# A TensorE warm-up, one lag moved to TensorE, late weights split earlier and a variance in column strips: a one-core residual block on Trainium2

## The chip, the cores and the metric

The kernel runs on one core of one Trainium2 chip. The time is the device time of one execution in microseconds (us). Three executions of the kernel before are given, and one further execution was profiled. TensorE (PE) multiplies, VectorE (DVE), ScalarE (ACT) and GpSimd (POOL) do the elementwise work, SyncE (SP) issues nearly all DMAs.

## The reference

The input x is 32 batches of 32 tokens with 256 channels, cond is 32 x 256. Two blocks follow each other:

```python
x = x + causal_depthwise_conv(x, w=cond)        # 32 taps (lags 0..31), one 256-wide tap per row of cond
ada = cond @ ada_w + ada_b                      # shift1, scale1, gate1, shift2, scale2, gate2
x1 = ln(x) * (1 + scale1) + shift1              # ln: mean and variance over 256 channels
attn_out = attention(x1 @ qkv_w + qkv_b)        # 16 heads of 128, 32 tokens per batch
y = x + gate1 * (attn_out @ out_w + out_b)
h = gelu((ln(y) * (1 + scale2) + shift2) @ ffn_w1 + ffn_b1)
return x + y + gate2 * (h @ ffn_w2 + ffn_b2)
```

## The kernel before

Channels lie on partitions: two channel tiles (`ct` 0 and 1) of 128 channels, and 1024 tokens in columns, in two halves of 512. The first half is handled in two quarters of 256 tokens through the first layer norm (`CHUNKS`, norms 0 and 1); norm 2 is the second half, norms 3 and 4 belong to the second block. Every engine has its own program written out by hand, and semaphores tie them together.

**Opening.** GpSimd makes the identity `ident` and the constant tile `ones` (1/256). TensorE transposes cond (L896), then the first half of x as it lands (L903); ScalarE and VectorE copy the transposes to `x0`. The convolution of a half is split: the lags in `PE_LAGS` go to TensorE as a product of x with a diagonal matrix of the tap (L917), the rest to VectorE as multiply-adds (L584). A lag j covers 16*(32-j) columns of a half. For the first half TensorE has lags 14 to 31 in the order 14, 31, 15, 30, ... 22, 23 and VectorE lags 0 to 13. The diagonals are made by ScalarE (L379) and GpSimd (L300). Each float32 product shows as two matmul instructions in the trace. Between lags TensorE also transposes the second half of x (L1093), makes the first modulation product (L969), and transposes the biases and the modulation rows. `conv_sum` (L598) adds TensorE's part to VectorE's; from it hang the mean, the squares, the variance, the reciprocal root (L316, a power on GpSimd), its spread over partitions (L961), and the first projection.

**Norm of a quarter.** TensorE's `var(n)` for n < 2 multiplies the squares, as weights, with a column of ones (L945); VectorE adds EPS (L628), GpSimd takes the power of a 128 x nt tile (L316), TensorE's `spread(n)` makes one product per 128 tokens. For n >= 2 the variance is made in strips of 32 partitions (L950), VectorE transposes 32 x 32 blocks (L630), adds EPS (L633), GpSimd takes the power of 128 x 4, and the spread is four products.

**Units.** Eight units U (two halves times four groups of four heads) follow: TensorE projects q, k, v (`project`), makes scores, attends with the probabilities of the unit before (`attend`, L1068) and projects out (`out_proj`). Weights are float32 split into a high part (ScalarE, `high_parts`, L374) and a low part (GpSimd, `low_parts`, L306). In unit 7 the weights of the feed-forward part are split the same way; the last two pieces (`late_raw`, held in `yacc`) are rounded by ScalarE after `exps(7)` (L503) and their low part is made by GpSimd after its loop over the units (L343). Then come `ffn1` and `ffn2`; ScalarE makes the gelu and `hh`, GpSimd and VectorE the low parts `hl` (L348, L843).

Of the kernel before, what the change touches and what calls it, by code (L numbers as in the profile page):

```python
# [5 lines left out]
F32 = mybir.dt.float32  # L6
F32R = mybir.dt.float32r
ALU = mybir.AluOpType
ACT = mybir.ActivationFunctionType
AX_X = mybir.AxisListType.X  # L10

P = 128
HALVES = 2
EPS = 1e-6


def cond_resid_block_kernel(nc, x, cond, ada_w, ada_b, qkv_w, qkv_b, out_w, out_b,
# [5 lines left out]
    B, T, C = x.shape  # L23
# [34 lines left out]

    PE_LAGS = [[lag for pair in zip(range(14, 23), range(31, 22, -1)) for lag in pair], list(range(14, 17))]
    DVE_LAGS = [[j for j in range(T) if j not in lags] for lags in PE_LAGS]
    DIAG_LAGS = PE_LAGS[0]
    ND = len(DIAG_LAGS) * CT
# [6 lines left out]
    with ExitStack() as ctx:  # L71
# [215 lines left out]
        @block.gpsimd  # L287
        def _(g):
            g.memset(ident[:, :], 0.0).then_inc(s_id0, 1)
            g.wait_ge(s_id0, 1)  # L290
            g.affine_select(out=ident[:, :], in_=ident[:, :], compare_op=ALU.not_equal, fill=1.0,
                            base=0, pattern=[[-1, P]], channel_multiplier=1).then_inc(s_const, 1)
            g.memset(ones[:, :], 1.0 / C).then_inc(s_const, 1)
            g.memset(mhalf[:, :], -0.5).then_inc(s_const, 1)
            g.wait_ge(s_const, 3)

            g.wait_ge(s_cond, 1)
            for d, ct in BY_POOL:
                j = DIAG_LAGS[d]
                g.tensor_scalar(diag[:, CT * d + ct, :], ident[:, :], condT[:, ct, T - 1 - j:T - j], 0.0,  # L300
                                ALU.mult, ALU.add).then_inc(s_diag[1], 1)

            def low_part(U, p):
                i, cols = p // 2, slice(PIECE * p, PIECE * (p + 1))
                g.wait_ge(s_whi[i], 2 * U + p % 2 + 1)
                g.tensor_tensor(wl[:, cols], raw[:, cols], wh[:, cols].bitcast(F32), ALU.subtract)\  # L306
                    .then_inc(s_wlo[i], 1)

            def low_parts(U, i):
                low_part(U, 2 * i)  # L310
                low_part(U, 2 * i + 1)

            def rstd(n):
                nt = NORMS[n][1] // P
                g.wait_ge(s_ve, n + 1)
                g.tensor_tensor(rs[:, 0:nt], ve[:, 0:nt], mhalf[:, 0:nt], ALU.pow).then_inc(s_rs, 1)  # L316


            g.wait_ge(s_in, CT)
            low_parts(0, 0)  # L320
            rstd(0)
            low_part(0, 2)
            g.wait_ge(s_lo, CT)
            low_part(0, 3)
            low_part(0, 4)
            rstd(1)
            low_part(0, 5)
            low_parts(0, 3)
            g.memset(pt[:, :, :, :], 0.0).then_inc(s_zero, 1)
            for i in range(3):  # L330
                low_parts(1, i)
            for U in range(1, NU):
                if U == 3:
                    rstd(2)
                if U == 5:
                    rstd(3)
                low_parts(U + 1, 0)
                low_parts(U + 1, 1)
                low_parts(U, 3)
                low_parts(U + 1, 2)  # L340
            for i in range(CT):
                g.wait_ge(s_latehi, i + 1)
                g.tensor_tensor(late_lo[:, i, :], late_raw[:, i, :], late_hi[:, i, :].bitcast(F32), ALU.subtract)\  # L343
                    .then_inc(s_latelo, 1)

            def hidden_low(n, m):
                g.wait_ge(s_hhi, MT * n + m + 1)
                g.tensor_tensor(hl[:, m, :], hf[:, m % 4, :], hh[:, m, :].bitcast(F32), ALU.subtract)\  # L348
                    .then_inc(s_hlo[0], 1)

            for m in (0, 2):
                hidden_low(0, m)

            g.wait_ge(s_mlo, CT * 3)
            for m in (4, 6):
                hidden_low(0, m)
            rstd(4)
            for m in (0, 2, 4, 6):
                hidden_low(1, m)

        @block.scalar
        def _(a):
# [85 lines left out]
            def o_high(U, h):  # L448
                a.wait_ge(s_pv, GH * U + h + 1)
                a.activation(oh[:, h, :], OB[h % 2][:, :], ACT.Identity, bias=bias(U, 2, h)).then_inc(s_ohi, 1)  # L450
# [21 lines left out]
            for U in range(1, NU):  # L472
                for j in range(4):
                    evac(U, j)
                if U == 1:

                    a.wait_ge(s_adap, 3)
                    a.wait_ge(s_adax, 1)
                    a.activation(ada_rows[:, :], S_BANK[:, 0:2 * P], ACT.Copy).then_inc(s_adac, 1)
                o_high(U - 1, 0)  # L480
                o_high(U - 1, 1)
                if U == 3:
                    squares(2)
                if U == 5:
                    squares(3)
                evac(U, 4)
                o_high(U - 1, 2)
                high_parts(U + 1, 0)
                o_high(U - 1, 3)
                if U == 3:  # L490
                    x1_high(2)
                if U == 5:
                    x1_high(3)
                for j in (5, 6, 7, 8):
                    evac(U, j)
                    if U in (2, 4) and j in (6, 7):
                        mean_high(U // 2 + 1, j - 6)
                high_parts(U + 1, 1)
                exps(U)
                if U == NU - 1:  # L500
                    a.wait_ge(s_late, 16 * CT)
                    for i in range(CT):
                        a.activation(late_hi[:, i, :], late_raw[:, i, :], ACT.Copy)\  # L503
                            .then_inc(s_latehi, 1)
                evac(U, 9)
                high_parts(U, 3)
                evac(U, 10)
                evac(U, 11)
                high_parts(U + 1, 2)
# [41 lines left out]
        def _(v):  # L551
# [71 lines left out]

            def var_eps(n):
                v.wait_ge(s_var, n + 1)
                if n < 2:
                    nt = NORMS[n][1] // P
                    v.tensor_scalar(ve[:, 0:nt], STAT_BANK[n][:, 0:nt], EPS, None, ALU.add).then_inc(s_ve, 1)  # L628
                else:
                    v.transpose(vt[:, :, :], STAT_BANK[n][:, 0:P].rearrange("p (k r) -> p k r", r=T))\  # L630
                        .then_inc(s_vt, 1)
                    v.wait_ge(s_vt, n - 1)
                    v.tensor_scalar(ve[:, :], vt[:, :, 0:1].rearrange("p k r -> p (k r)"), EPS, None, ALU.add)\  # L633
                        .then_inc(s_ve, 1)

            def norm(n):
                v.wait_ge(s_rb, n + 1)
# [252 lines left out]

        @block.tensor
        def _(pe):
            pe.wait_ge(s_const, 1)
            pe.wait_ge(s_row[0], 16)
            for ct in range(CT):
                m = pe.transpose(S_BANK[:, B * ct:B * (ct + 1)], crow[:, ct * P:(ct + 1) * P], ident[0:B, 0:B])  # L896
# [1 line left out]
            for n in range(2):  # L898
                t0, nt = CHUNKS[n][0] // P, CHUNKS[n][1] // P
                pe.wait_ge(s_x[n], 16)  # L900
                for ct in range(CT):
                    for t in range(nt):
                        m = pe.transpose((OB, YB)[n][ct][:, t * P:(t + 1) * P], xtok[:, t0 + t, ct * P:(ct + 1) * P], ident[:, :])  # L903
                m.then_inc(s_xt, 1)

            def conv(n, i0, i1):
                last = len(PE_LAGS[n]) - 1
# [31 lines left out]

            def var(n):  # L940
                pe.wait_ge(s_sq, CT * (n + 1))
                if n < 2:
                    for t in range(NORMS[n][1] // P):
                        for ct in range(CT):
                            m = pe.matmul(STAT_BANK[n][:, t:t + 1], ln_sq(n, ct)[:, t * P:(t + 1) * P],  # L945
                                          ones[:, 0:1], start=(ct == 0), stop=(ct == CT - 1))
                else:
                    for ct in range(CT):
                        for t in range(TG):
                            m = pe.matmul(STAT_BANK[n][T * t:T * (t + 1), 0:P], ones[:, 0:T],  # L950
                                          ln_sq(n, ct)[:, t * P:(t + 1) * P], start=(ct == 0), stop=(ct == CT - 1))
                m.then_inc(s_var, 1)

            def spread(n):
                pe.wait_ge(s_rs, n + 1)
                for k in range(NORMS[n][1] // P):
                    if n < 2:
                        dst = STAT_BANK[n][:, k * P:(k + 1) * P]
                    else:
                        dst = STAT_BANK[n][:, :].rearrange("p (t k r) -> p k t r", t=TG, r=T)[:, k]  # L960
                    m = pe.matmul(dst, rs[:, k:k + 1].to_broadcast([P, P]), ident[:, :], start=True, stop=True)  # L961
                m.then_inc(s_rb, 1)

            def modulation(i):
# [323 lines left out]
```

## Time and profile before

| what | value |
|---|---|
| three runs | 311.98, 313.19, 313.54 us, median 313.19 |
| profiled execution, its own time | 314.73 us |
| its span, first to last instruction | 312.9 us |
| TensorE busy | 302.3 us, 97% of the span, 2604 matmul instructions |
| VectorE, ScalarE, GpSimd busy | 177.7, 174.4, 119.5 us |
| mean granted TensorE clock | 0.998 |

The profiled execution's time is 1.83 us above its span, and 1.54 us above the median of the three runs. Busy times are sums over the whole span; they don't tell which wait ends last in a stage. The start of an instruction in the timeline is where it begins, and the distance between two starts is what one costs in a dense stream; its own duration also holds a tail that the next one overlaps.

### The profile page before, as it was taken

The page shows a single profiled execution, that of the slowest core. Times are in us where ns is not written, and L with a number is a line of the kernel's source. Part 1 is how long each engine was busy: PE and PEld are TensorE (multiplying, and loading weights), DVE is VectorE, ACT ScalarE, POOL GpSimd, SP SyncE. Part 2 cuts the span into 40 slices and gives each one's busy share as a digit, 9 for nine tenths or more (in the row PEclk, how much of TensorE's full clock was granted, in tenths as well). Part 3 has the DMA queues.
Part 4 walks back from the last instruction along what each step waited for, and adds up shares of the span by engine and source line. Part 5 has one row for each costly group of instructions (what it writes and reads, how often), then busy time and mean ns, then how long its engine had stood idle before and what let it go on. Part 6 is the DMA issues. An engine that isn't in the chain of part 4 may idle for free.

```text
span 312.9 us, 6154 instructions
## 1 busy us (share of the span) xinstructions
PE 302.3 (97%) x2604; PEld 255.2 (82%) x2604; DVE 177.7 (57%) x304; ACT 174.4 (56%) x316; POOL 119.5 (38%) x103
## 2 busy tenths in 40 slices
PE   4998999999999999999999999999999989999995
PEld 3896897887888888888888888888898868878885
DVE  3985798888768555453446553340620555757232
ACT  5454567543762856376367636644762793725901
POOL 5105646630823364064327224630911492311400
PEclk9999999999999999999999999999999999999999
DMA  6902240600080052007003400520180000000012
GB/s 216 374 24 65 71 136 2 196 7 0 3 270 0 2 164 107 1 4 266 3 2 112 159 2 2 180 90 0 33 304 2 2 0 3 0 0 1 2 67 67
DMA packets 15275, 23.00 MB, mean 74 GB/s; under 512 B 808, under 2 KB 8336, under 8 KB 15248
## 3 DMA queue, kind: packets, MB, share of 16 engines
q1 hardware_dynamic: 15200, 22.58, 21.4%
q8 instruction: 20, 0.33, 0.4%
q14 instruction: 7, 0.06, 0.1%
q10 hardware_dynamic: 48, 0.03, 0.0%
HBM read 21.57 MB, written 1.05 MB: 72 GB/s over the span
## 4 chain that ended last, share of the span: by engine, by line
PE 87%; DVE 5%; ACT 4%; POOL 2%; DMA 1%; issue 1%; DVEq 0%
PE bank L981 15%; PE bank L983 15%; PE bank L982 15%; PE bank L1068 8%; PE bank L917 5%; PE bank L989 4%; PE bank L991 4%; PE bank L990 4%; PE bank L1052 3%; PE bank L1191 2%; PE bank L1193 2%; PE bank L1192 2%; POOL wl L306 1%; PE bank L961 1%; ACT wh L374 1%; DVE xc L584 1%
## 5 line engine op out<-in xcount | busy, mean ns | idle before, releaser
L306 POOL TENSOR_TENSOR wl<-raw,wh 128x512 fp32r<-128x512 f32 x70 | 94.9, 1381 | 129.7 <-ACT wh L374 110.9
L425 ACT ACTIVATE pool<-bank,bT 128x512 f32<-128x512 f32 x56 | 38.5, 688 | 54.4 <-PE bank L983 54.4
L981 PE MATMUL bank<-x1h,wl 128*128 128x512 f32 (+1 forms) x174 | 65.6, 377 | 0.5 <-POOL wl L306 0.5
L982 PE MATMUL bank<-x1l,wh 128*128 128x512 f32 (+1 forms) x174 | 64.6, 371 | 0.0
L983 PE MATMUL bank<-x1h,wh 128*128 128x512 f32 (+1 forms) x174 | 64.6, 371 | 0.0
L707 DVE SCALAR_TENSOR_TENSOR ol<-bank,bT,oh 128x512 fp32r<-128x512 f32 x32 | 24.0, 750 | 37.4 <-ACT oh L450 36.3
L584 DVE SCALAR_TENSOR_TENSOR xc<-x,condT,xc 128x496 f32<-128x496 f32 (+27 forms) x82 | 43.3, 597 | 0.1
L374 ACT ACTIVATE wh<-raw 128x512 fp32r<-128x512 f32 x70 | 39.8, 622 | 0.0
L981 PEld LDWEIGHTS bank<-x1h,wl 128*128 128x128 f32 x174 | 32.8, 189 | 6.5 <-POOL wl L306 1.0
L983 PEld LDWEIGHTS bank<-x1h,wh 128*128 128x128 f32 x174 | 32.7, 188 | 5.7
L982 PEld LDWEIGHTS bank<-x1l,wh 128*128 128x128 f32 x174 | 32.8, 188 | 5.3
L1068 PEld LDWEIGHTS bank<-pt,pool 128*128 128x128 f32 x256 | 32.1, 191 | 3.7 <-issue 1.9
L1068 PE MATMUL bank<-pt,pool 128*128 128x128 f32 x256 | 32.5, 275 | 1.5 <-DVE ol L707 1.5
L450 ACT ACTIVATE oh<-bank,bT 128x512 fp32r<-128x512 f32 x32 | 22.0, 687 | 10.9 <-PE bank L1068 10.9
L981 PE MATMUL bank<-oh,wl 128*128 128x512 f32 x64 | 26.7, 418 | 0.2 <-DVE ol L707 0.2
L989 PE MATMUL bank<-wh,x1l 128*128 128x512 f32 x64 | 25.9, 405 | 0.0
L983 PE MATMUL bank<-oh,wh 128*128 128x512 f32 x64 | 25.1, 392 | 0.0
L991 PE MATMUL bank<-wh,x1h 128*128 128x512 f32 x64 | 25.0, 391 | 0.0
L982 PE MATMUL bank<-ol,wh 128*128 128x512 f32 x64 | 25.0, 390 | 0.0
L990 PE MATMUL bank<-wl,x1h 128*128 128x512 f32 x64 | 25.0, 390 | 0.0
L702 DVE STREAM_TRANSPOSE pt<-pnorm 32x512 f32<-32x512 f32 (+1 forms) x36 | 23.2, 644 | 1.2
L679 DVE TENSOR_REDUCE mx<-bank 128x16 f32<-128x512 f32 x8 | 5.5, 692 | 32.2 <-PE bank L1052 32.2
(136 smaller groups left out, 432.4 us busy)
## 6 DMA issues: line engine op xcount, KB each, us to landing
raw<-in_L_cond_qkv_w_dram SPq DMA_DIRECT2D x24, 512.0 KB, 5.6
raw<-in_L_cond_out_w_dram SPq DMA_DIRECT2D x8, 512.0 KB, 3.5
raw<-in_L_cond_ffn_w_dram SPq DMA_DIRECT2D x3, 512.0 KB, 6.2
adaw<-in_L_cond_ada_w_dram SPq DMA_DIRECT2D x1, 1024.0 KB, 10.6
out_dram<-pool SPq DMA_DIRECT2D x3, 256.0 KB, 2.2
xtok<-in_x_dram SPq DMA_DIRECT2D x2, 256.0 KB, 3.1
adaw<-in_L_cond_ada_w_dram SPq DMA_DIRECT2D x1, 512.0 KB, 5.7
xtok<-in_x_dram SPq DMA_DIRECT2D x1, 512.0 KB, 6.5
```

The source lines that it names most:

```text
L306: g.tensor_tensor(wl[:, cols], raw[:, cols], wh[:, cols].bitcast(F32), ALU.subtract)\
L374: a.activation(wh[:, cols], raw[:, cols], ACT.Copy).then_inc(s_whi[i], 1)
L425: a.activation((q_sb if j < GH else k_sb)[:, j % GH, :], src, ACT.Identity, bias=bias(U, j // GH, j % GH)).then_inc(s_ev, 1)
L584: m = v.scalar_tensor_tensor(out=acc[:, :, j:], in0=xs[:, :, :T - j], scalar=w, in1=(acc if i else xs)[:, :, j:], op0=ALU.mult, op1=ALU.add)
L707: v.scalar_tensor_tensor(out=ol[:, h, :], in0=OB[h % 2][:, :], scalar=bT[:, row:row + 1], in1=oh[:, h, :].bitcast(F32), op0=ALU.add, op1=A ...
L981: pe.matmul(dst, wl[:, w_cols], a_hi, start=start, stop=False)
L982: pe.matmul(dst, wh[:, w_cols], a_lo, start=False, stop=False)
L983: return pe.matmul(dst, wh[:, w_cols], a_hi, start=False, stop=stop)
L989: pe.matmul(dst, x1l[:, kt, tk], wh[:, wc], start=(kt == 0), stop=False)
L990: pe.matmul(dst, x1h[:, kt, tk], wl[:, wc], start=False, stop=False)
L991: m = pe.matmul(dst, x1h[:, kt, tk], wh[:, wc], start=False, stop=(kt == CT - 1))
L1068: m = pe.matmul(OB[h % 2][:, t * P:(t + 1) * P], v_sb[:, t, h * P:(h + 1) * P], pt[:, h, t, :], start=True, stop=True)
```

## The change

Four edits: lag 13 of the first half moves from VectorE to TensorE and the order of TensorE's lags becomes 13, 31, 14, 30, 15, ... 23, 22; TensorE makes four products of the constants before the first transposes and three behind the transposes of x, into a bank that is read by nobody then; the late weights are split earlier in unit 7 on ScalarE and GpSimd; norm 1 (the second quarter) takes the variance and its spread by the way of norms 2 to 4.

```diff
-    PE_LAGS = [[lag for pair in zip(range(14, 23), range(31, 22, -1)) for lag in pair], list(range(14, 17))]
+    PE_LAGS = [[13] + [lag for pair in zip(range(31, 22, -1), range(14, 23)) for lag in pair], list(range(14, 17))]
 ...
             def rstd(n):
                 nt = NORMS[n][1] // P
+                at = (slice(0, P), slice(0, nt)) if n == 0 else (slice(0, T * nt), slice(0, TG))
                 g.wait_ge(s_ve, n + 1)
-                g.tensor_tensor(rs[:, 0:nt], ve[:, 0:nt], mhalf[:, 0:nt], ALU.pow).then_inc(s_rs, 1)
+                g.tensor_tensor(rs[at], ve[at], mhalf[at], ALU.pow).then_inc(s_rs, 1)
 ...
                 low_parts(U + 1, 0)
+                if U == NU - 1:
+                    for i in range(CT):
+                        g.wait_ge(s_latehi, i + 1)
+                        g.tensor_tensor(late_lo[:, i, :], late_raw[:, i, :], late_hi[:, i, :].bitcast(F32),
+                                        ALU.subtract).then_inc(s_latelo, 1)
                 low_parts(U + 1, 1)
                 low_parts(U, 3)
                 low_parts(U + 1, 2)
-            for i in range(CT):
-                g.wait_ge(s_latehi, i + 1)
-                g.tensor_tensor(late_lo[:, i, :], late_raw[:, i, :], late_hi[:, i, :].bitcast(F32), ALU.subtract)\
-                    .then_inc(s_latelo, 1)
 ...
                 o_high(U - 1, 3)
+                if U == NU - 1:
+                    a.wait_ge(s_late, 16 * CT)
+                    for i in range(CT):
+                        a.activation(late_hi[:, i, :], late_raw[:, i, :], ACT.Copy)\
+                            .then_inc(s_latehi, 1)
 ...
                 high_parts(U + 1, 1)
                 exps(U)
-                if U == NU - 1:
-                    a.wait_ge(s_late, 16 * CT)
-                    for i in range(CT):
-                        a.activation(late_hi[:, i, :], late_raw[:, i, :], ACT.Copy)\
-                            .then_inc(s_latehi, 1)
 ...
             def var_eps(n):
                 v.wait_ge(s_var, n + 1)
-                if n < 2:
+                strips = T * (NORMS[n][1] // P)
+                if n == 0:
                     nt = NORMS[n][1] // P
                     v.tensor_scalar(ve[:, 0:nt], STAT_BANK[n][:, 0:nt], EPS, None, ALU.add).then_inc(s_ve, 1)
                 else:
-                    v.transpose(vt[:, :, :], STAT_BANK[n][:, 0:P].rearrange("p (k r) -> p k r", r=T))\
+                    v.transpose(vt[0:strips], STAT_BANK[n][0:strips, 0:P].rearrange("p (k r) -> p k r", r=T))\
                         .then_inc(s_vt, 1)
-                    v.wait_ge(s_vt, n - 1)
-                    v.tensor_scalar(ve[:, :], vt[:, :, 0:1].rearrange("p k r -> p (k r)"), EPS, None, ALU.add)\
-                        .then_inc(s_ve, 1)
+                    v.wait_ge(s_vt, n)
+                    v.tensor_scalar(ve[0:strips, :], vt[0:strips, :, 0:1].rearrange("p k r -> p (k r)"), EPS, None,
+                                    ALU.add).then_inc(s_ve, 1)
 ...
-            pe.wait_ge(s_const, 1)
+            def idle_products(count):
+
+                for _ in range(count):
+                    pe.matmul(PB[1][:, 0:P], ident[:, :], ones[:, :], start=True, stop=True)
+
+            pe.wait_ge(s_const, 2)
+            idle_products(4)
 ...
                 m.then_inc(s_xt, 1)
+            idle_products(3)
 ...
             def var(n):
                 pe.wait_ge(s_sq, CT * (n + 1))
-                if n < 2:
+                if n == 0:
 ...
                 else:
                     for ct in range(CT):
-                        for t in range(TG):
+                        for t in range(NORMS[n][1] // P):
 ...
             def spread(n):
                 pe.wait_ge(s_rs, n + 1)
-                for k in range(NORMS[n][1] // P):
-                    if n < 2:
-                        dst = STAT_BANK[n][:, k * P:(k + 1) * P]
+                nt = NORMS[n][1] // P
+                for k in range(nt if n == 0 else TG):
+                    if n == 0:
+                        dst, rows_n = STAT_BANK[n][:, k * P:(k + 1) * P], P
                     else:
-                        dst = STAT_BANK[n][:, :].rearrange("p (t k r) -> p k t r", t=TG, r=T)[:, k]
-                    m = pe.matmul(dst, rs[:, k:k + 1].to_broadcast([P, P]), ident[:, :], start=True, stop=True)
+                        dst = STAT_BANK[n][:, 0:P * nt].rearrange("p (t k r) -> p k t r", t=nt, r=T)[:, k]
+                        rows_n = T * nt
+                    m = pe.matmul(dst, rs[0:rows_n, k:k + 1].to_broadcast([rows_n, P]), ident[0:rows_n, 0:rows_n],
+                                  start=True, stop=True)
                 m.then_inc(s_rb, 1)
```

## Rows read from the trace of the kernel before

**Rows 1.** The page: shares of the chain that ended last, by engine.

```profile
PE 87%; DVE 5%; ACT 4%; POOL 2%; DMA 1%; issue 1%; DVEq 0%
```

**Rows 2.** Timeline of the opening: start us, duration us, engine, line, tiles.

```profile
1.42 0.20 POOL L293 MEMSET ones<- 128x128 f32 x1
6.04 5.36 ACT L379 ACTIVATE diag<-ident,condT 128x128 f32<-128x128 f32 x18
20.67 0.54 DVE L584 SCALAR_TENSOR_TENSOR xc<-x,condT,xc 128x320 f32<-128x320 f32 x1
24.89 0.95 DVE L598 TENSOR_TENSOR xc<-xc,bank 128x144 f32<-128x144 f32 x4 [2.79 <-PE bank L917]
```

**Rows 3.** Timeline of TensorE, 5 to 19 us, single instructions.

```profile
6.33 0.85 PE L917 MATMUL bank<-x,diag 128*128 128x288 f32 x1 [0.60 <-DVE x L564]
7.45 0.69 PE L917 MATMUL bank<-x,diag 128*128 128x288 f32 x1
7.93 0.69 PE L917 MATMUL bank<-x,diag 128*128 128x288 f32 x1
9.12 0.80 PE L917 MATMUL bank<-x,diag 128*128 128x272 f32 x1
14.37 0.44 PE L1093 MATMUL bank<-ident,xtok 128*128 128x128 f32 x1
16.89 0.61 PE L917 MATMUL bank<-x,diag 128*128 128x240 f32 x1
18.32 0.41 PE L917 MATMUL bank<-x,diag 128*128 128x224 f32 x1
```

**Rows 4.** Windows: stretch, busy of each engine (instructions), granted clock, DMA share, GB/s.

```profile
10.00:15.00 5.00, 5.00 (x18) 4.29 (x18) 5.00 (x9) 1.40 (x5) 0.00 (x0) 1.00 1.04 386
```

**Rows 5.** Timeline of TensorE, 19 to 30 us.

```profile
19.64 0.64 PE L969 MATMUL bank<-adaw,condT 128*32 128x128 f32 x16
28.10 1.05 PE L945 MATMUL bank<-ones,x 128*128 128x1 f32 x8 [0.47 <-ACT x L405]
29.56 0.39 PE L917 MATMUL bank<-x,diag 128*128 128x272 f32 x1
29.80 0.39 PE L917 MATMUL bank<-x,diag 128*128 128x272 f32 x1
```

**Rows 6.** Timeline of the second quarter's norm.

```profile
36.28 0.15 DVE L628 TENSOR_SCALAR ve<-bank 128x2 f32<-128x2 f32 x1
36.51 0.70 POOL L316 TENSOR_TENSOR rs<-ve,mhalf 128x2 f32<-128x2 f32 x1 [0.43 <-DVE ve L628]
37.26 0.52 PEld L961 LDWEIGHTS bank<-ident,rs 128*128 128x128 f32 x4 [0.35 <-POOL rs L316]
```

**Rows 7.** Timeline and chain, the same steps in norm 4.

```profile
276.18 0.31 DVE L630 STREAM_TRANSPOSE vt<-bank 128x128 f32<-128x128 f32 x1
276.77 1.01 POOL L316 TENSOR_TENSOR rs<-ve,mhalf 128x4 f32<-128x4 f32 x1 [3.17 <-DVE ve L633]
...
278.56 0.89 PE bank L961 x8
```

**Rows 8.** Timeline of unit 7 and the step into ffn1.

```profile
240.02 0.69 ACT L425 ACTIVATE pool<-bank,bT 128x512 f32<-128x512 f32 x1 [4.76 <-PE bank L983]
245.30 2.56 POOL L306 TENSOR_TENSOR wl<-raw,wh 128x512 fp32r<-128x512 f32 x2 [9.19 <-ACT wh L374]
247.32 1.14 ACT L503 ACTIVATE late_hi<-yacc 128x512 fp32r<-128x512 f32 x2
255.92 1.67 DVE L843 TENSOR_TENSOR hl<-pool,hh 128x512 fp32r<-128x512 f32 x1 [3.03 <-ACT hh L519]
258.40 1.13 PE L1068 MATMUL bank<-pt,pool 128*128 128x128 f32 x8 [1.54 <-DVE ol L707]
275.57 0.69 DVE L843 TENSOR_TENSOR hl<-pool,hh 128x512 fp32r<-128x512 f32 x1 [0.55 <-ACT hh L519]
```

**Rows 9.** Windows (columns as in the windows group above), after the late weights' loads.

```profile
234.00:236.00 2.00, 2.00 (x13) 1.71 (x13) 0.71 (x1) 0.72 (x2) 2.00 (x2) 1.00 0.01 3
```

## The prediction, made before the changed kernel was run

> **What bounds the kernel now.** I read the page first. TensorE is busy for 97% of the span, and of the chain that ended last it holds 87% [rows 1]. So time is won in two ways only: TensorE does less (or does it faster), or it waits less. Next I read its waits. There are few, and two bear on this change: the 1.54 us before the third `attend` of unit 7 at 258.40, put down to VectorE's `ol` [rows 8], and 0.35 us before the spread of the second quarter [rows 6]. Last I read the opening instruction by instruction, because half of the change sits there.
>
> In the opening the reader should compare distances between starts. Two 288-column instructions start 0.48 us apart at 7.45 and 7.93 [rows 3]; two 272-column ones start 0.24 us apart at 29.56 and 29.80 [rows 5]. Per column that is 1.67 ns against 0.88 ns: TensorE runs at its lower level (1.2 GHz) early and at 2.4 GHz later. At 16.89 a 240-column instruction still lasts 0.61 us, at 18.32 a 224-column one lasts 0.41 us [rows 3], so the level rises in between, about 18.0. The granted clock of 10 to 15 us reads 1.00 all the same [rows 4]; for this stretch the durations decide, not that column. The Trainium skill (TensorE: Matmul & The Clock Gate, Part 1) says the lower clock is the default and activity releases it; that agrees with the durations and not with the granted clock.
>
> The opening ends with TensorE: VectorE's last wide multiply-add of lag 12 starts at 20.67, it then does the two of lag 13 (0.46 us each by the distance between such starts), and idles 2.79 us for TensorE until 24.89 [rows 2]. All that follows hangs from `conv_sum`, on every engine, so a shift of it goes through to the end undiminished unless a later wait takes it; the waits left on TensorE are too small to take it.
>
> **Edit 1: products of constants, and lag 13.** The first four products need `ones`, ready at 1.62 [rows 2]; eight instructions of 128 columns at 1.67 ns a column are 8 x 0.213 = 1.7 us, to about 3.4. That is where TensorE starts on cond now. Cost: 0 to 0.1 us. The second group starts when the x transposes are through. The engine was idle for 0.60 us before 6.33 [rows 3], the tail of 0.2 us counts as free too, and six instructions are 1.28 us: the convolution starts at about 6.8 instead of 6.33. Cost 0.5 us at the lower level.
>
> What they may buy is the rise of the clock. Before, it rose inside a dense stretch that began with the transposes at 14.37; in front of it, the wide lags were broken by narrow ones (lag 31, 16 columns, has its four instructions from 7.93 + 0.48 = 8.41 to 9.12, 0.18 us each, in which hardly anything streams) and by the idle 0.60 us [rows 3]. With the change the stretch from 1.7 to 8.8 is dense but for some 0.3 us at 3.5: products, transposes, products, then the 304 columns of lag 13. The longest dense stretch so far is shorter than this one. I let the rise fall at 7.8, one microsecond behind the convolution's new start and well inside the dense part; bounds 5 and 9, its middle and its end.
>
> TensorE's work of the opening at the upper level: the wide lags 13 to 23 have 16 x (19+18+...+9) = 2464 columns per tile; four instructions each at 0.88 ns a column give 8.7 us. The eight narrow lags 24 to 31 go at the floor; eight one-column instructions took 1.05 us with a tail, so 0.12 us each [rows 5], 4 x 0.12 x 8 = 3.8 us. Between them: eight transposes at 0.12 (1.0), the modulation product (0.6) [rows 5], two small turns (0.2). Sum 14.3 us. From 6.8 that ends at 21.1; one microsecond at the lower level in front (to 7.8) does half its work, so 21.6. Here lag 13 itself is 304 x 4 x 0.88 = 1.07 us of TensorE.
>
> VectorE loses the two multiply-adds of lag 13 and is through at 20.67 + 0.54 = 21.2. So TensorE still ends last, at 21.6 against 24.89 before: **-3.3 us**. With a rise at 5, VectorE's 21.2 to 21.3 binds: -3.6. With a rise at 9 it is 22.2: -2.7. ScalarE's diagonals, now 28 for 27, are at hand: 18 of them are made by 11.4 [rows 2], and the last eight follow the second half's copies, some 2.4 us of work behind transposes that come two microseconds earlier. Were they late, TensorE would wait for lags 25 and on; I price that at 0 and name it below.
>
> **Edit 2: the late weights.** ScalarE's two conversions take 1.14 us at 247.32 (1.04 without the tail), in front of the last copies, the conversions of `w2` and the first gelu. Moved behind `o_high(6, 3)` they fall into the 4.76 us in which ScalarE waits before 240.02 [rows 8]. Their loads have landed by then: the DMA moves 3 GB/s from 234 to 236 [rows 9]. On GpSimd the two subtractions leave the place before `hidden_low(0, 0)` and fall into the wait between `low_parts(8, 0)` and 245.30. Two subtractions of their form take 2.56 us there, the wait is 9.19 us [rows 8]. Nothing else queues behind either new place before 240.
>
> Effect on the stall: ScalarE's whole chain comes 1.04 us earlier, and VectorE's `hl` of tile 1, which took 1.67 us at 255.92 beside GpSimd's work and takes 0.69 us alone at 275.57 [rows 8], should take nearer to 0.7. Together up to 2.0 us, more than the 1.54 us of idle at 258.40, so the stall goes: **-1.6 us** (the 0.1 is the start of a stream after a wait). Bounds: -1.0 if only ScalarE's part counts, -1.7. Late next is the projection of head 2, which needs an `ol` with more than 1 us to spare. If the cover before 240 were gone, 1.04 us of ScalarE would hit the copy of tile 5.
>
> **Edit 3: second quarter's variance in strips.** TensorE's own variance product gets cheaper than the 1.05 us of eight one-column instructions (norm 0's, of the same form [rows 5]), but behind it TensorE waits 0.35 us for the reciprocal root anyway [rows 6], so a saving there only lengthens that wait: 0. The path is VectorE, GpSimd, spread. VectorE's EPS ran at 36.28, not because of TensorE but behind its own modulation multiplies. Now a block transpose goes in front. In norm 4 the power starts 0.59 us after the transpose starts [rows 7], here 0.23 us after EPS [rows 6]: +0.36. The power of 128 x 4 takes 1.01 us [rows 7], that of 128 x 2 0.70 [rows 6]; the new one is 64 x 4. Both rows have all partitions, so the cost follows the columns: +0.30, bound 0 from below if 64 partitions cost half. The spread becomes four products of 64 columns, eight instructions; four products of 128 columns took 0.89 [rows 7], two take half of it, 0.45: +0.43, and 0 from below if the narrow ones pair up. Sum **+1.1 us** on the path, bounds +0.3 and +1.2. Behind the spread TensorE streams without a break for 10 us, so nothing absorbs it; the next waits there are for steps that follow TensorE themselves.
>
> **Sum.** -3.3 - 1.6 + 1.1 = -3.8 us. The profiled execution would go from 314.73 to 310.9, its span from 312.9 to 309.1. The profiled time stands 1.54 us over the median; against that median of 313.19 it is **309.4 us**.
>
> **Rivals.** A change of 0.5% (1.6 us) is about what a measurement of this kernel can tell from none.
>
> A, the clock rises no earlier (slower). Durations before show a full 2 us of 288 columns after transposes without a rise. Then six lags at the lower level from 6.8: 864 wide columns x 4 x 1.67 = 5.8, three narrow lags 2.1, to 14.7; transposes 1.7, lag 16 1.7, rise at 18.1; the rest (1344 columns 4.7, five narrow 2.4, others 0.8) ends at 26.0, +1.1 against 24.89, or +2.6 if the rise slips another 3 us. Net +0.6 to +2.1, **314.5 us**. It decides when the rise comes after 15.4: there 21.1 + 8.6/2 = 25.4 eats the 0.5 that edits 2 and 3 leave. Chance 0.13.
>
> B, the rise comes earlier, but only near 12, because the transposes break the stretch. 21.1 + 2.6 = 23.7, -1.2, net -1.7: **311.5 us**. Against it: before, the rise came right behind eight transposes. Chance 0.12. Beside it stands a rule of the Trainium skill (TensorE: Matmul & The Clock Gate, Part 4): a transpose doesn't count as activity. By it the dense part would begin at 5.5 with the second products; the transposes in front of the rise at 18.0 speak against that rule.
>
> C, the stall at 258.40 stays or half stays, since the `ol` behind it waits for something else: net -2.2 to -3.2, **310.5 us**. Chance 0.08.
>
> D, the strips cost nothing (the order of GpSimd's low parts shifts, or the narrow spread is quick): -4.9, **308.3 us**. Chance 0.12.
>
> My forecast keeps 0.55, with its own range 308.4 to 310.4. The range over cases leaves out A and little else: 307.8 to 311.6. Faster by over 0.5% (under 311.6): the forecast, C, D, and half of B, 0.81; within: the other half of B and half of A, 0.12; slower: 0.07.
>
> **What would show it.** Edit 1: starts of TensorE's instructions in lag 13 to 15 spaced 0.25 us instead of 0.5, `conv_sum` near 21.6, VectorE's idle before it under 0.5 us. Edit 2: `late_hi` near 232, no idle before the third `attend` of the last unit, VectorE's `hl` of tile 1 at 0.7 us. Edit 3: a power of 1.0 us and TensorE idle of 1 us or more before the spread, which then takes 0.9 us. I am wrong if the lower level lasts beyond 12 us, if diagonals come late for lag 25 and on, or if another wait grows between 25 and 60 us by what the opening gave.

## The result, and the profile after

| | kernel before | changed kernel |
|---|---|---|
| median of 20 runs | 312.16 us (311.95 to 313.70) | 313.69 us (312.58 to 315.50) |
| ratio to before, over all executions | | 1.0038, 95% interval 1.0022 to 1.0055 |
| profiled execution, its span | 314.73, 312.9 us | 314.52, 312.6 us |

Ratios are taken over all executions, so they differ a little from the quotient of two medians. One execution, 428.0 us at a mean granted clock of 0.657 in the run with two tiny products, was in a slower state, and its ratio leaves it out.

I had forecast 309.4 us in a range of 307.8 to 311.6. The change makes the kernel a little slower. The two profiled spans are equal within 0.3 us, so the first question is whether the forecast gains are there. They are. The timeline of the opening in the changed kernel:

```profile
7.01 0.42 PE L927 MATMUL bank<-x,diag 128*128 128x304 f32 x1
7.26 0.42 PE L927 MATMUL bank<-x,diag 128*128 128x304 f32 x1
21.65 0.98 DVE L600 TENSOR_TENSOR xc<-xc,bank 128x152 f32<-128x152 f32 x4
```

304 columns now cost 0.25 us from start to start, the upper level from the first lag on (it starts at 6.75), where 288 columns took 0.48 [rows 3]. The products of constants just before start 0.21 us apart up to 6.2 us and 0.11 us apart from 6.4 on, so the clock rose at about 6.3. The sum of the convolution starts at 21.65, not 24.89 [rows 2]: 3.24 us earlier. It carries no idle bracket: VectorE, not TensorE, ends last, and TensorE waits for it 1.7 us.

The second quarter's norm, from the same view:

```profile
33.06 0.30 DVE L633 STREAM_TRANSPOSE vt<-bank 64x128 f32<-64x128 f32 x1
33.63 1.00 POOL L317 TENSOR_TENSOR rs<-ve,mhalf 64x4 f32<-64x4 f32 x1 [0.78 <-DVE ve L636]
34.69 1.10 PE L973 MATMUL bank<-ident,rs 64*128 64x64 f32 x8 [1.13 <-POOL rs L317]
```

The answers to [rows 6]: the transpose stands in front, the power takes 1.00 us on half the partitions, as on all of them, TensorE waits 1.13 us for it, and from the spread's start to the next product it is 1.03 us (34.69 to 35.72) where it was 0.47 (37.26 to 37.73). And the last unit:

```profile
236.52 1.14 ACT L495 ACTIVATE late_hi<-yacc 128x512 fp32r<-128x512 f32 x2
237.45 2.52 POOL L342 TENSOR_TENSOR late_lo<-yacc,late_hi 128x512 fp32r<-128x512 f32 x2
256.60 0.69 DVE L846 TENSOR_TENSOR hl<-pool,hh 128x512 fp32r<-128x512 f32 x1 [2.33 <-ACT hh L521]
258.10 1.13 PE L1081 MATMUL bank<-pt,pool 128*128 128x128 f32 x8
```

Against [rows 8], VectorE's `hl` takes 0.69 us instead of 1.67, and the 1.54 us of idle in front of TensorE's third `attend` is gone. ScalarE converts the late weights at 236.52, not near 232 as forecast, but still inside its wait, which shrinks from 4.76 to 3.73 us. Now the place where the gains were lost. In the timeline of TensorE there is a hole in unit 3, two matmuls before the end of the scores:

```profile
131.57 1.28 PE L1065 MATMUL bank<-pool 128*32 128x32 f32 x126
134.79 0.22 PE L1065 MATMUL bank<-pool 128*32 128x32 f32 x2 [1.94 <-issue]
...
162.19 1.30 PE L1065 MATMUL bank<-pool 128*32 128x32 f32 x128
```

The windows of the stretch behind it (busy of each engine, then the granted clock, DMA share, GB/s):

```profile
136.00:138.00 2.00, 2.00 (x7) 1.51 (x5) 1.27 (x3) 1.50 (x3) 0.00 (x0) 0.52 0.00 0
138.00:140.00 2.00, 2.00 (x7) 1.63 (x6) 1.90 (x4) 1.14 (x3) 1.79 (x2) 0.62 0.03 8
```

126 of 128 matmuls run, then TensorE stands for 1.94 us for nothing the profile shows ("issue"), then the last two run. After that wait the granted clock falls to its lower level for some 3.4 us. From these scores to the next unit's it is 30.6 us (131.57 to 162.19); in the kernel before (133.97 to 160.81) and in a later run without a hole it is 26.8. So the hole and the clock behind it cost 3.8 us in this execution. Of the 20 runs, seven had a mean granted clock of 1.0 and took 312.6 to 312.9 us, ten had 0.995 (313.5 to 314.7), three 0.989 (315.4 to 315.5): the clock does not fall every time, and seems to fall twice in some. Where it fell is seen only in the profiled one. The waits of the opening can do the same, as a run below shows, so not every fall need come from the hole.

With the hole in, the two profiles add up. Opening -3.2; strips +0.8 (from the sum of the convolution to unit 1's scores, 53.5 us for 52.7); unit 3 to unit 4 +3.8; from unit 4's scores to the end, with the late weights, -1.7 (150.5 us for 152.1). That is -0.3 us, and the spans are 312.6 and 312.9.

### The profile page after: what moved, and what is told of

The parts are those of the page before. It is cut to its first block, busy times and chain, and to the rows that moved or that the text cites. A ratio compares the mean times of both kernels' runs of the same rounds, so it can differ in the third digit from the quotient of the medians.

```text
span 312.6 us, 6198 instructions
## 1 busy us (share of the span) xinstructions
PE 302.2 (97%) x2626; PEld 255.3 (82%) x2626; DVE 176.2 (56%) x303; ACT 174.5 (56%) x317; POOL 120.0 (38%) x104
## 3 DMA queue, kind: packets, MB, share of 16 engines
HBM read 21.57 MB, written 1.05 MB: 72 GB/s over the span
## 4 chain that ended last, share of the span: by engine, by line
PE 86%; DVE 8%; POOL 2%; ACT 2%; issue 1%; DVEq 0%; POOLq 0%
PE bank L994 16%; PE bank L996 15%; PE bank L995 15%; PE bank L1081 9%; DVE xc L586 5%; PE bank L1002 5%; PE bank L1004 5%; PE bank L1003 5%; PE bank L1065 3%; PE bank L1204 2%; PE bank L1206 2%; PE bank L1205 2%; PE bank L973 1%; POOL wl L306 1%; PE bank L940 1%
## 5 line engine op out<-in xcount | busy, mean ns | idle before, releaser
L586 DVE SCALAR_TENSOR_TENSOR xc<-x,condT,xc 128x496 f32<-128x496 f32 (+27 forms) x80 | 42.1, 595 | 0.1
L994 PE MATMUL bank<-oh,wl 128*128 128x512 f32 x64 | 26.8, 418 | 0.2 <-DVE ol L710 0.2
L1004 PE MATMUL bank<-wh,x1h 128*128 128x512 f32 x64 | 25.7, 402 | 0.0
```

The costliest lines, as they stand in the source:

```text
L586: m = v.scalar_tensor_tensor(out=acc[:, :, j:], in0=xs[:, :, :T - j], scalar=w, in1=(acc if i else xs)[:, :, j:], op0=ALU.mult, op1=ALU.add)
L994: pe.matmul(dst, wl[:, w_cols], a_hi, start=start, stop=False)
L1004: m = pe.matmul(dst, x1h[:, kt, tk], wh[:, wc], start=False, stop=(kt == CT - 1))
```

## The experiments

A *tiny product* below is this, one float32 product into a bank nobody reads then. It stands as four instructions in TensorE's program (two weight loads, two matmuls), so it moves all that follows by four places and takes little time:

```python
pe.matmul(PB[1][0:32, 0:32], ident[:, 0:32], ones[:, 0:32], start=True, stop=True)
```

The kernel before was timed again beside these runs; its medians lie between 312.0 and 312.1 us.

**Two tiny products in front of the first four products (changed kernel otherwise).**

> The changed kernel with two tiny products (128x32 by 32 columns, eight TensorE instructions with their weight loads) put in front of the four products of constants; nothing else. Theory 1, code loading: the 1.94 us hole in unit 3's scores and the lower clock behind it come from a 256-instruction piece of TensorE's code that ends two matmuls before the 256-instruction burst of scores does; eight instructions more put the border inside the burst, so the hole and the clock drop vanish and the span falls by 1.9 to 3.8 us, to about 309 us, device time near 310.7. Theory 2, the products or the strips disturb unit 3 by timing or power: nothing moves, 312.6 to 315.

Median 312.95 us (before: 312.0), ratio 1.0008 (0.9982 to 1.0034). Timeline of its unit 3:

```profile
131.85 1.25 PE L1067 MATMUL bank<-pool 128*32 128x32 f32 x122
134.82 0.26 PE L1067 MATMUL bank<-pool 128*32 128x32 f32 x6 [1.73 <-issue]
```

My size was wrong: the hole stayed, at 1.73 us. Its place was right: eight instructions more in front moved it by four matmuls and their four weight loads. In both kernels it stands in front of TensorE's 1233rd matmul. It sits at a fixed place of the program's code, not at a fixed work step. In this profile the clock did not fall, and to the next scores it is 28.8 us, 1.9 more than without a hole.

**The kernel before with 44 instructions more, and nothing of the change.**

```diff
-            pe.wait_ge(s_const, 1)
+            pe.wait_ge(s_const, 2)
+            for _ in range(11):
+                pe.matmul(PB[1][0:32, 0:32], ident[:, 0:32], ones[:, 0:32], start=True, stop=True)
```

> The kernel before with eleven tiny products (44 TensorE instructions) ahead of the wait for cond; nothing of the change is in it. Theory 1 (code loading): its scores of unit 3 stand where those of the changed kernel stand in TensorE's code, so a hole of 1.9 us appears there, often with a stretch at the lower clock: 1.9 to 3.8 us slower than before. Theory 2: no difference to before beyond 0.3 us, or a small gain if the tiny products raise the clock earlier.

Median 314.88 us against 312.0, ratio 1.0066 (1.0041 to 1.0091); the fastest execution is 2.2 us above the fastest of the kernel before (314.04, 311.81). Timeline:

```profile
131.19 1.28 PE L1054 MATMUL bank<-pool 128*32 128x32 f32 x126
134.41 0.22 PE L1054 MATMUL bank<-pool 128*32 128x32 f32 x2 [1.94 <-issue]
```

The same hole at the same matmul and with the same length, in a kernel with none of the four edits. This settles where the hole comes from: the change's 22 more matmul instructions, each with its weight load (2626 for 2604, so 44 places), are enough, whatever they compute. The page's queue of instructions agrees in size: 20 packets with 0.33 MB in the kernel before, 21 in the changed one, so about 16 KB of code a packet; the 5208 matmuls and weight loads of the kernel before are 20.3 pieces of 256. The Trainium skill (Runtime: NRT & Kernel Launch, Instruction fetch mechanics) says engines refill code in 16 KiB blocks of 256 instructions, which agrees; it also calls the crossing mostly hidden, and of some twenty crossings here one is not. One unit's scores are 256 instructions in 1.3 us. When a border of the pieces lies a few instructions in front of them, the whole next piece is used up before the one after it is there.

The trace also has the time of each packet of that queue. In the four profiles with a hole (this one, the changed kernel, the runs before and after this one) a 16 KB packet starts 0.5 to 0.6 us into the scores of unit 3, and TensorE goes on 2.3 to 2.7 us after its start (132.07 and 134.79 in the changed kernel). In front of unit 4 of the changed kernel the packet starts at 160.66, 1.5 us ahead of the scores, and there is no hole. The unchanged kernel has a packet 0.7 us into unit 3's scores too, but there the 1233rd matmul comes 20 matmuls behind them. That TensorE waits for this packet is read from these times; the profile names no releaser.

**The old variance of the second quarter, four tiny products in front.**

> The changed kernel with the second quarter's variance and spread as before (one-column products, a power of 128x2, two spreading products), and four tiny products in front so that the later code stands exactly as in the run with two tiny products. My theory: the strips cost 1.1 us on the path from the reciprocal root to the spread, so this is 1.1 us faster than that run, near 309.6. Rival: the strips are free or gain, no difference or slower.

Median 312.18 us, ratio 0.9990 (0.9969 to 1.0011), 0.8 us below the run with two tiny products, at the same code place and with the same hole behind 122 matmuls (1.64 us). I had expected 1.1. From the sum of the convolution to unit 1's scores it is 52.7 us here and 53.5 there, 0.8.

**The kernel before with the late weights' edit alone.**

> The kernel before with the late weights' edit alone; TensorE's code is as before. My theory: the 1.54 us idle of TensorE in the last unit goes, 1.5 to 1.7 us faster than before, span 311.3 in a profile like that of before. Rival: half of it stays, 0.8 us.

Median 310.90 against 312.0 us, ratio 0.9945 (0.9922 to 0.9968), which is 1.7 us. The medians are only 1.1 apart, but both the fastest and the slowest executions are 1.7 apart (310.13 and 312.88 against 311.81 and 314.59), and in the profiles it is 150.3 us from unit 4's scores to the end instead of 152.1. The third `attend` of the last unit in its timeline has no idle in front:

```profile
254.10 1.13 PE L1069 MATMUL bank<-pt,pool 128*128 128x128 f32 x8
```

**Eight tiny products behind the three products of constants: the code moves by 32.**

> The changed kernel with eight tiny products behind the three products of constants: TensorE's later code moves by 32 instructions. Theory 1 (code loading): the run with two tiny products moved the hole by exactly four matmuls and kept it, since the piece of code still starts less than 3 us before the scores; with 32 the piece starts about 4 us before them, the hole goes in every unit, 1.9 us less and no lower clock in unit 3: about 310.9 us. Rival: the hole moves again by 16 matmuls and stays near 1.7 us, or another unit gets one: 312.6.

Median 310.86 against 312.09 us, ratio 0.9954 (0.9935 to 0.9973), as expected. The timeline shows the scores of unit 3 whole:

```profile
132.71 1.30 PE L1067 MATMUL bank<-pool 128*32 128x32 f32 x128
```

In its trace no packet of code starts between 124.94 and 134.51. So the changed kernel, with its four edits untouched and its code moved, goes from 313.69 to 310.86: the code's place was worth 2.8 us. The seven executions of the changed kernel without a fall of the clock (312.6 to 312.9) lie 1.9 us above 310.86, which is the hole alone. Four of its twelve runs took 311.8 to 311.9, at a mean granted clock of 0.993 or 0.994. The profile is of one of those, and its windows show where: the granted clock falls behind the two waits of the opening (1.4 us for the sum of the convolution, 1.1 us for the spread of the strips).

```profile
36.00:38.00 2.00, 2.00 (x11) 2.00 (x11) 2.00 (x3) 0.00 (x0) 2.00 (x2) 0.50 0.38 88
```

**The same with the old variance** (ten tiny products; the later code stands at the same place).

> As the run with eight tiny products, with the second quarter's variance and spread as before and ten tiny products, so that the later code stands at the same place. My theory: the strips cost 0.8 to 1.1 us on the path, so about 309.9 us, and below the kernel before by 2 us. Rival: strips free, no difference to the other run.

Median 309.97 us (309.83 to 310.29 in six runs), ratio 0.9916 (0.9885 to 0.9947). The strips cost 0.9 us by the medians.

**The same without the products of constants** (17 tiny ones behind x).

> As the last, without the seven products of constants (tiny products keep the code at its place); lag 13 stays on TensorE. Theory A: the products raise the clock early; without them the convolution runs at the lower level for a time that differs from execution to execution, the sum of the convolution comes between 21.3 and 26, and the times spread over 3 us with a median 1 us or more above. Theory B: the clock rises early in most executions anyway; median equal or 0.3 us lower, since cond and x are transposed 0.3 us sooner.

Median 310.20 us, 309.64 to 310.89, ratio 0.9922. This tells little: the 17 tiny products themselves ran for 1.5 us in the place of the others, and in the profile the clock rose among them, at about 6.6 us (their instructions start 0.053 us apart, then 0.032), before lag 13. It wasn't a kernel without products.

**The same as the run with ten tiny products, lag 13 back on VectorE, old order of lags** (twelve tiny products).

> As the run with the old norm, with lag 13 back on VectorE and the old order of lags: products, late weights and shifted code only. If VectorE bounds the opening once the clock is high, the sum of the convolution comes 0.9 us later (near 22.5) and the time is 0.9 us longer than with lag 13 moved. Rival: TensorE bounds it, no difference.

Median 311.53 us, ratio 0.9979 (0.9956 to 1.0002), 1.56 us more than with lag 13 moved. The sum of the convolution starts at 22.42 instead of 21.74, 0.7 us. The rest is again the clock: TensorE now waits longest, and the mean's products behind that wait run slow (1.54 us where they take 1.10); from 24 to 26 us the windows read 0.50. The one execution of twelve at a mean clock of 0.999 took 310.73, 0.8 above 309.97.

```profile
22.42 0.94 DVE L600 TENSOR_TENSOR xc<-xc,bank 128x144 f32<-128x144 f32 x4
23.09 1.54 PE L948 MATMUL bank<-xc,ones 128*128 128x256 f32 x4 [2.36 <-DVE xc L600]
```

**Three products in front, three behind, eleven tiny ones in the wait before the mean; old variance.**

```diff
-            idle_products(4)
+            idle_products(3)
...
             conv(0, 16, len(PE_LAGS[0]))
+            for _ in range(11):
+                pe.matmul(PB[1][0:32, 0:32], ident[:, 0:32], ones[:, 0:32], start=True, stop=True)
```

> Lag 13 on TensorE, late weights early, the old variance of the second quarter; three products of constants in front instead of four, three behind, and the eleven tiny products that place the code stand in the wait before the mean. With four in front, VectorE's work began 0.3 us later than without; with three TensorE is free when cond lands, so the sum of the convolution comes near 21.4 and the time is 0.2 to 0.3 us below the 309.97 of the run with four, near 309.7. Rival: a shorter dense stretch lets the clock rise later in some executions and the median rises above 310.

Median 309.37 us (309.32 to 309.63 in six runs) against 312.10, ratio 0.9885 (0.9851 to 0.9920): the fastest of all, 1.15% below the kernel before. I had expected 309.7; the sum starts at 21.34, as expected:

```profile
21.34 0.98 DVE L600 TENSOR_TENSOR xc<-xc,bank 128x152 f32<-128x152 f32 x4
```

**No product before the convolution at all** (17 tiny ones in the wait before the mean, otherwise as the last).

> The same without any product of constants before the convolution (in the run that left them out before, seventeen tiny ones stood there and the clock was up by 8). Theory A, the products raise the clock: now the convolution starts at the lower level, which ends anywhere between 9 and 18 us, the sum of the convolution comes at 21.3 to 25, times spread over 309.7 to 313, median 1 us or more above the run with three and three. Theory B, they do nothing: same median within 0.3 us.

Median 312.56 us, from 310.71 to 314.65, ratio 0.9983 (0.9950 to 1.0017): 3.2 us above the run with three and three, and spread over 4 us where that one spreads over 0.3. Its timeline shows the lower level through lag 13 and most of lag 14, and TensorE late:

```profile
7.50 0.71 PE L925 MATMUL bank<-x,diag 128*128 128x304 f32 x1
11.70 0.39 PE L925 MATMUL bank<-x,diag 128*128 128x272 f32 x1
22.27 0.98 DVE L600 TENSOR_TENSOR xc<-xc,bank 128x152 f32<-128x152 f32 x4 [0.95 <-PE bank L925]
```

So the products do what they seem to be for: theory A holds. About 0.5 of the 3.2 us is the tiny products' own, though: TensorE is late here, they stand in the way, and the mean's first product starts 1.28 us behind the sum (22.27 to 23.55) where it was 0.68 (21.34 to 22.02). And the products pay only together with lag 13. Lag 13 moved without products took 312.56, products without lag 13 moved 311.53, and neither of the two, in the run with the late weights alone, 310.90; both together took 309.97 and 309.37. (These runs differ in their tiny products too.) In the seven profiles with six or seven products the clock rose between 5.3 and 7.0 us; in five without, apart from the run with 17 tiny ones in their place, between 10.5 and 18.0.

**The kernel before once more.**

> The kernel before once more for its profile. If the moment at which the clock rises differs from execution to execution, TensorE's convolution in this profile ends near 22.1 to 22.5 instead of 24.8, and the sum of the convolution starts within 0.5 us of VectorE's last multiply-add; span about 310.2. If the first profile was typical, the sum starts at 24.9 again.

```profile
15.82 0.37 PE L917 MATMUL bank<-x,diag 128*128 128x240 f32 x1
23.59 0.95 DVE L598 TENSOR_TENSOR xc<-xc,bank 128x144 f32<-128x144 f32 x4 [1.47 <-PE bank L917]
```

At 16.89 the first profile still had 0.61 us for a 240-column instruction [rows 3]; here it is 0.37 at 15.82. The clock rose some 2.5 us earlier, the sum came at 23.59, and the execution took 313.29 us: 1.44 less than the first profile's 314.73, for 1.30 us of earlier sum. The eight runs took 311.8 to 313.3. Neither of my two numbers was hit; the answer lies between. In the profile of the late weights alone, whose opening is the same, the sum came at 22.49. All 76 executions of the kernel before beside the experiments fall into three groups, 311.8 to 312.4, 313.1 to 313.5 and 314.6 to 314.8 (six of them): the first profile belongs to the slowest.

## Why the prediction was wrong

**What failed is a step that isn't in it.** The prediction priced what each edit adds or moves in time, and said that a shift of `conv_sum` "goes through to the end undiminished unless a later wait takes it". It never asked what 44 more instructions in front do to the code behind them. They moved a border of the pieces in which TensorE's code is loaded to a few instructions before the scores of unit 3. That put in a wait of 1.94 us, which no row of before could show, and in the profiled execution the clock fell behind it: 2.8 us between the medians 310.86 and 313.69, of which 1.9 are the hole and the rest a lower clock, at the hole or in the opening. That the place of the code makes the hole is shown by two runs from both sides (44 instructions alone bring it, 32 more remove it).

**The second failure is the baseline.** "The profiled execution would go from 314.73 to 310.9 ... against that median it is 309.4": I carried a difference measured in one execution over to the median, and took the opening's 24.89 for typical. The median itself, 313.19 of three executions, was 1.0 above the 312.16 of twenty. That profiled execution is slower than all 20 runs of the kernel before (at most 313.70). The clock rose at 18.0 in it, at about 15.4 in the second profile. An execution of 311.8 us is 1.5 below that second profile, and its sum would lie 1.5 us earlier, at 22.1, just where VectorE ends (21.57 plus its 0.52); that is an estimate from these two profiles. So the edit of the opening was worth 3.2 us against the profile I had and far less against the median: 0.9 us by the runs (310.90 for the late weights alone, 309.97 with the products and lag 13), and 0.3 between the fastest executions of the two (310.13, 309.83). It mostly takes away the slow openings.

**Point by point.**

- The opening: sum of the convolution forecast at 21.6, measured 21.65. The mechanism was right (rival A, no earlier rise, and rival B, transposes break the stretch, both fell). Two sizes were off and cancelled, so the near hit is luck in part: the rise came before 6.75, so TensorE was done at 20.6 and not 21.6, and the products in front cost 0.3 us, not 0 to 0.1. They delayed cond and with it VectorE, which I had at 21.2 and which ended at 21.6: not TensorE but VectorE bound the opening. Three products instead of four, and the tiny ones moved, gave 0.6 us.
- The late weights: forecast -1.6, measured -1.7. Rival C fell.
- The strips: forecast +1.1, bounds +0.3 and +1.2, measured +0.9. Each piece was there: transpose in front, power of 1.00 us by its four columns, 1.13 us of idle, a spread of eight instructions. To unit 0's scores they cost 1.2 us (27.0 from the sum of the convolution for 25.8), to unit 1's 0.8. In between the kernel before waits 0.54 us for a low part of GpSimd at 54.08, and no kernel with strips has that wait: "nothing absorbs it" was wrong by 0.4 us. Rival D fell.
- Sum against the median with the measured sizes: -0.9 - 1.7 + 0.9 = -1.7, which is 310.5; the changed kernel with its code moved took 310.86. The sum mixes medians with a ratio: with the 1.1 between the medians for the late weights it is -1.1, and 311.1. The 2.8 us of the code's place bring 310.86 to the measured 313.7.

**What stays open.** What decides when a packet of code starts: with eight instructions more in front it still started 0.6 us into the scores, while for unit 4 of the changed kernel, at nearly the same distance from a border, it started 1.5 us ahead of them. And why the clock falls in some executions behind a wait of 1 to 2 us and not in others.

## What to carry to other kernels

Adding or removing instructions on an engine with dense bursts moves every later burst against the borders of code loading. After such a change look for idle of "issue" in the middle of one burst, and move the code by some tens of cheap instructions in a wait before judging the change; otherwise a gain of 1.2 us is read as a loss of 1.5. Take more than one profile of the kernel before: if the clock rises at a different time in each, only runs tell what the opening costs. And fill, or avoid, waits of TensorE over 1 us: they cost their length, and sometimes a stretch at the lower clock.

## What the runs showed of the hardware

- TensorE stood still for 1.94 us two matmuls before the end of a 256-instruction burst, in two different kernels with equally many instructions ahead of it; with eight more in front it stood still at the same instruction number, four matmuls earlier in the burst. A 16 KB packet of code had started 2.3 to 2.7 us before it went on.
- With lag 13 on TensorE, six products of constants in an otherwise idle engine took 3.2 us off the median (0.5 of it the fillers' own) and cut the spread of the times from 4 us to 0.3 us.
- The granted clock column read 1.00 while durations showed the lower level at the start of a kernel; later falls, behind waits of 1.1 to 2.4 us, did show in it, as 0.50 to 0.65.
- GpSimd's power takes 1.00 us on 64x4 as on 128x4, and 0.70 on 128x2: its cost follows the columns.
